# Writing out every round of a graph-attention kernel's edge stages, in place of loops over four rounds

## The reference

```python
xh = (h @ W).reshape(n, heads, d)
a_s = (xh * att_src).sum(-1); a_d = (xh * att_dst).sum(-1)
alpha = leaky_relu(a_s[src] + a_d[dst], 0.2)
amax = segment_max(alpha, dst)
e = exp(alpha - amax[dst])
alpha = e / (segment_sum(e, dst)[dst] + 1e-16)
out = segment_sum(xh[src] * alpha[:, :, None], dst)
```

## Time and profile before

| what | value |
|---|---|
| time, median of 3 runs | 9329.89 us (9316.76 to 9336.9) |
| the profiled execution's own time | 9341.26 us |
| its span, first to last instruction | 9339.6 us |
| busy: PE / PEld / DVE / ACT / POOL | 56% / 39% / 59% / 19% / 56% of the span |
| mean granted TensorE clock | 0.726 of full speed |
| edge stages, windows 0 to 82 | about 250 to 2860, 3040 to 5670, 5860 to 8480 us |

### The profile page before, as it was taken

How to read it: one execution, slowest core, us unless ns; L and a number is a source line. 1 busy time by engine, 2 the same in 40 slices (tenths; PEclk the granted TensorE clock), 3 DMA queues, 4 the chain that set the end, 5 groups by cost and what they waited for, 6 DMA issues and landing times. The chain is left out here.

```text
span 9339.6 us, 122620 instructions
## 1 busy us (share of the span) xinstructions
PE 5257.9 (56%) x21872; PEld 3686.3 (39%) x21873; DVE 5523.9 (59%) x14694; ACT 1794.4 (19%) x6145; POOL 5226.3 (56%) x5539
## 2 busy tenths in 40 slices
PE   4256565555556255555655556266666655553497
PEld 2144444433334144444433334144444443333255
DVE  4356565655558366666665658356666666558543
ACT  2011111110103022222210102122222221012333
POOL 3566666666662566666666662566666666661332
PEclk7577777776767577777776766677777777666699
DMA  3344444444442344444443333344444443334333
GB/s 119 115 141 134 140 136 138 141 133 135 135 132 87 110 117 119 117 118 119 118 118 112 110 113 109 109 118 127 123 123 122 125 123 111 111 112 136 106 54 76
DMA packets 541784, 1107.22 MB, mean 119 GB/s; under 512 B 125282, under 2 KB 333647, under 8 KB 541155
## 3 DMA queue, kind: packets, MB, share of 16 engines
q0 software_dynamic: 274368, 731.65, 29.1%
q1 hardware_dynamic: 265811, 370.32, 12.2%
q10 hardware_dynamic: 1152, 1.05, 0.0%
HBM read 962.72 MB, written 148.65 MB: 119 GB/s over the span
## 5 line engine op out<-in xcount | busy, mean ns | idle before, releaser
L1126 POOL DMA_INDIRECT edges_G<-rows,edges_index x4980 | 4767.6, 957 | 2943.5 <-issue 1374.7
L1320 PE MATMUL edges_ps_o<-edges_G,edges_OH 128*128 128x264 f32 x9960 | 3617.4, 516 | 2804.4 <-DVE acc L1584 1660.1
L1320 PEld LDWEIGHTS edges_ps_o<-edges_G,edges_OH 128*128 128x128 f32 x9960 | 2347.7, 252 | 3769.9 <-DVE acc L1584 1761.1
L1584 DVE TENSOR_TENSOR acc<-acc,edges_ps_o 128x264 f32 x2490 | 1057.2, 425 | 1934.0 <-remote 897.5
L1566 DVE TENSOR_TENSOR edges_G<-edges_G,edges_ps_c 128x1024 f32<-128x1024 f32 x1245 | 1501.5, 1206 | 56.6 <-ACT edges_G L1154 48.8
L1145 ACT ACTIVATE edges_node<-terms 128x12 bf16 x2490 | 494.5, 210 | 2463.1 <-issue 2432.5
L1558 DVE TENSOR_TENSOR edges_OH<-edges_ps_c,relT 128x512 f32<-128x512 f32 x1245 | 847.4, 681 | 37.5 <-issue 25.0
L1153 ACT ACTIVATE edges_ps_c<-edges_diff 128x80 f32<-128x80 f32 x249 | 60.0, 241 | 2316.3 <-DVE edges_diff L1546 2153.2
L2403 POOL DMA_INDIRECT x<-experts_Y,experts_token x105 | 162.1, 1544 | 373.1 <-issue 213.5
L1479 DVE TENSOR_TENSOR_SCAN edges_run<-edges_masks,edges_ps_s 128x128 f32<-128x128 bf16 x249 | 102.9, 413 | 424.1 <-ACT edges_fade L1163 256.4
L1278 PEld LDWEIGHTS edges_ps_s<-edges_node,edges_OHT 128*128 128x128 bf16 x4980 | 180.4, 103 | 209.0 <-issue 178.9
(11 more groups left out here) (345 smaller groups left out, 6340.4 us busy)
## 6 DMA issues: line engine op xcount, KB each, us to landing
edges_rels<-rel SPq DMA_DIRECT2D x249, 640.0 KB
edges_G<-rows,edges_index POOLq DMA_INDIRECT x4980
xslot<-edges_blank SPq DMA_DIRECT2D x80, 650.0 KB
edges_masks<-lanes SPq DMA_DIRECT2D x249, 96.0 KB
rows<-node_ext POOLq DMA_DIRECT2D x147, 130.0 KB, 2.4
experts_X<-xslot SPq DMA_DIRECT2D x105, 130.0 KB, 2.1
node_rows<-rows SPq DMA_DIRECT2D x98, 130.0 KB, 2.1
edges_xm<-xn SPq DMA_DIRECT2D x98, 128.0 KB
```

Source lines behind the costliest of these rows:

```text
L1126: g.indirect_dma_start(G[n][:, s, 0:RW], None, dr["rows"], bass.IndirectOffsetOnAxis(index[n][:, s:s + 1], 0)).then_inc(gathered[n], 16)
L1320: mm = pe.matmul(ps_o[BANK_OF[g]][:, 0:GW], OH[:, 2 * g + j, :], G[n][:, 2 * g + j, :], start=(j == 0), stop=(j == 1))
L1584: v.tensor_tensor(a, a, ps_o[BANK_OF[g]][:, 0:GW], ALU.add).then_inc(added, 1)
```

## The change

`over_windows` loses its loops: it calls `step` for every window with numbers for `i` and `n`, on all five engines and in all three layers. `step` and everything below it stay as they are. Windows that ran as passes of a loop are now instructions of their own with constant addresses and constant wait values. The register work that depends on data (the block numbers) stays.

```diff
-        def over_windows(eng, step, ahead, early, mixes=True):
-
-            rounds = (NW - ahead) // RING
-
-            def unrolled(a, z):
-                for w in range(a, z):
-                    step(w // RING, w % RING, mixes)
-
-            def looped(a, z, mix):
-                with eng.Fori(a, z) as i:
-                    for n in range(RING):
-                        step(i, n, mix)
-
-            if mixes:
-                unrolled(-early, RING * FILLED)
-                looped(FILLED, FULL, True)
-                unrolled(RING * FULL, RING * DRAINED)
-                looped(DRAINED, rounds, False)
-            else:
-                unrolled(-early, RING)
-                looped(1, rounds, False)
-            unrolled(RING * rounds, NW)
+        def over_windows(step, early, mixes=True):
+
+            for w in range(-early, NW):
+                step(w // RING, w % RING, mixes)
...
-            over_windows(sp, step, RING, 3)
+            over_windows(step, 3)
...
-            over_windows(g, step, 0, 0, False)
+            over_windows(step, 0, False)
...
-            over_windows(a, step, 1 + RING, 1)
+            over_windows(step, 1)
...
-            over_windows(pe, step, 3, 3)
+            over_windows(step, 3)
...
-            over_windows(v, step, 3, 3)
+            over_windows(step, 3)
```

## The result

| | median | lowest to highest | runs |
|---|---|---|---|
| before | 9331.09 us | 9316.76 to 9336.9 | 4 |
| changed | 9215.05 us | 9213.99 to 9216.71 | 4 |

The account below looks back on a forecast made before the run. No engine is full; DVE, PE and ACT drive each other in turn. Second loop 33 plus first loop 54 gives 87 us off 9341.3, so 9254 us, or 9242 us on the runs' scale; range 9180 to 9320 us.

Parts of the forecast that it names:

- First loop, 54 us: Windows 8 to 47 of each layer, 40 windows: gain of 54 us, the middle between 31 and 78 us.
- Second loop, 33 us: Last 24 windows per layer, going to the rate of windows 48 to 55: gain of 33 us.
- the others may settle nearer to DVE: Rival, all of DVE's saving returns in a long run without loops: 8965 to 9218 us; gain over 150 us gets 6%.
- Windows 3 to 7 and 48 to 55, nothing: Stretches already written out for PE, DVE, ACT and SP: no gain counted in the sum.
- POOL and the others at nothing: POOL's loop costed at nothing for its slack (30.3 against 25.0 us); written-out rates already include PE, ACT and SP.
- The back edge: DVE's idle time ahead of L1546, 112.1 us, mostly at 42 loop jumps of 2.44 us each, vanishes; mostly absorbed.
- The register instructions: DVE's address and threshold work in looped windows: 0.6 us per window at two lines, as much again elsewhere; mostly absorbed.
- ACT's wait about as before: ACT's 2432 us of idle time ahead of L1145, the copies of `load_node`, stays about as before.
- A gain over 150 us: Rival for the whole run, with all of DVE's saving coming back: 6%.
- no gain: Rival: waiting for ACT's `load_node` takes up all the saving and the time stays 9330 us; 7%.
- The fetch: Rival: written-out code stalls for instruction fetch on DVE, ACT and PE, 120 us more, 9450 us; slower gets 7%.
- The bound I named and did not use: POOL's gathers at 25.0 us per window would bound the kernel if its cover went, 5 us below the forecast rate.

Follow-up runs that it names:

- the hint: The kernel before, all loops kept, with VectorE's loops alone told to fetch the back edge's branch target in advance: 9358.74 us, ratio 1.0015.

## Why the prediction was right, and where it wasn't

**The sum.** *First loop, 54 us:* measured 56.4. The middle between the two written-out rates came out right in size, which is luck: the prediction had no reason for either side. *Second loop, 33 us:* 54.1 in 23 windows, and 51.5 with that loop alone changed; this is the mis-sized term. I took the rate of windows 48 to 55 for its goal, but these stood between two loops and follow the last mix work; a long stretch without loops settles at 29.88 to 30.06. The rival that said so ("the others may settle nearer to DVE") was right in kind and far too large in size. *Windows 3 to 7 and 48 to 55, nothing:* 8.9 and 2.9 us. I had called their streams already written out; POOL's was not.

**POOL and the others at nothing.** "It has slack, so I cost its part at nothing" was wrong for windows 3 to 7, where the kernel with VectorE left looped already has the gain; in the second loop it nearly held (30.08 us on average with POOL looped, 29.97 without). The engines beside VectorE bring 55 of 116 us. "Its rate includes it" was true of the written-out rates, but I didn't see from it that half of the gain would not be VectorE's.

**The back edge.** The idle time vanished as said (112.1 to 13.8 us), but nothing shows that it was worth anything: with two thirds of the stall removed alone, the time stayed (1.0015). "Most is absorbed" was, as far as measured, "all". (Of the 46 cases in the earlier trace rows 40 are back edges, not 42; two more end with PE.)

**The register instructions.** I had sized VectorE's at 1.2 us per looped window, by their medians. The ordinary ones that went took 1.1 us; those over 0.6 us, which I saw in the earlier trace rows and did not count, took another 3.1 us (587 us in 192 windows). The sum didn't stand on this, since it went by rates. That the gain lies in these long ones is argued from what went, not shown by a run of its own.

**ACT's wait about as before.** This was wrong: 2432 to 1605 us, with the same instructions in number. I took the wait for work on data that stays, and did not look at the spread of one instruction's duration. Of the 4731 that compute block numbers, 1213 are slow before, 1113 with VectorE alone written out, 1030 with the others and 832 with all; but with the hint, which takes no register work away, they are 1303 and the wait is 2597 us, so a hundred more or less is the scatter between two kernels. VectorE's own slow ones don't fall when the others are written out (935 to 954). That an engine is slowed less when others do less register work is thus shown for ScalarE and the whole change alone, and what couples them is not shown.

**The rivals.** A gain over 150 us and no gain both fell on the chip of the first measurement. The fetch: no cost of it shows. Two queues of the page carry instructions. q8 has 61 packets before and 168 in every kernel with PE written out throughout, PE alone included, so it is PE's. q14 has the others': 392 packets before, 395 after, 434 with POOL alone and 459 with ScalarE alone written out, but 276 with VectorE alone:

```profile
q14 instruction: 276, 2.26, 0.1%
```

VectorE's loops thus fetched more than its written-out code does, 116 packets net, or 2.8 per back edge. The "issue" idle time ahead of PE's matmuls and VectorE's additions fell. Among the larger waits it grew at four places: ahead of PE's weight loads at L1302 (1571 to 1633 us), ScalarE's L1135, told above, and in the same way L1225 (94 to 255 us in 19 cases, otherwise put down to VectorE), and between POOL's gathers (1375 to 1540 us in 4474 pieces, 0.34 us each). By the rule of the Trainium skill, Runtime: NRT & Kernel Launch, section Instruction fetch mechanics, 112 us would have come back; 116 us did, but the kernel with the hint shows that this is a coincidence: it removed most of the stall and gained nothing. That crossing a block is mostly hidden agrees with the trace: in the changed kernel on the third chip no idle time of VectorE's edge stages that ended with "issue" is over 2 us.

**The bound I named and did not use.** POOL's 25.0 us per window is the pace on three other chips, at 7857 to 7877 us. There the change loses 0.2%. The forecast holds where register instructions are slow at times, as in the profile that it was read from; nothing in that profile says that they aren't so everywhere.

**Open:** what makes register instructions take 0.7 us on the first chip and never on the three others, and whether it belongs to the chip or to the time; which engine beside VectorE carries the other 55 us; what the last third of the back edge's stall is worth; and whether pauses between gathers would help where instructions are slow. Back edges of the other engines explain little of the 55 us: their sequencers lose 43 us in the whole run behind them, all four together. No kernel here beats the changed one on the first chip, or the one before on the others.

## What to carry to other kernels

Compare the rate of the same step, looped and written out, within one trace before adding up stalls, and take the rate of a long stretch; a stall ahead of a wait on another engine can be worth nothing, however plain its row (69 us of it taken out in two layers here, 0 gained). Look at the longest duration of a register instruction beside its median, and if they are far apart (1637 ns against 38), measure at another time and on another chip before tuning against it. Where a loop's register work is off the pace-setting engine, as beside POOL's 25 us per window of gathers here, writing it out brings nothing and can cost.

## What the runs showed of the hardware

- The same kernel takes 9331 to 9346 us in two measurements and 7857 to 7877 us on three other chips, each measured at one time. A window takes 30.7 us in the one and 25.05 us in the other. The mean granted TensorE clock is 0.73 and 0.78 to 0.79. It is no general slowness: an addition into `acc` takes 424 ns and a register instruction 38 ns at the median in both.
- A register instruction has a second duration of about 0.7 us, up to 1.6 us, against 38 ns, on ScalarE, VectorE and SyncE alike, not on PE and POOL. It goes with long rows of gathers on POOL (82% of ScalarE's after eight and more), but only on the first chip; on the three others it never came.
- After a taken back edge of VectorE's loop, whose pass is 468 recorded instructions, some 2.9 us pass before the sequencer's next one, on the second chip too. For ScalarE (240), POOL (126) and SP (100) it is 0.21 to 0.23 us, for PE (some 440) 0.06 us. A prefetch hint takes VectorE's to 0.2 to 0.5 us in layers 0 and 2, but only to 1.7 to 3.1 us in layer 1.
- An indirect gather of 128 rows takes POOL 0.95 us, and the next starts 0.3 us later: 25.05 us per 20, where POOL sets the pace.
